# An adaLN block with attention and top-1 experts: GpSimd is drained between the two stages and behind the sends of the first five pairs

## The reference

```python
h = _layernorm(x, axis=-1) * (1 + ca) + sa
x = x + ga * _L0_attn_ref(h, w_qkv, w_swiglu, w_out)      # q, k, v, exp(k), cumsums, gated product
h = _layernorm(x, axis=-1) * (1 + cb) + sb
x = x + gb * _L0_ffn_ref(h, gate_w, w1, w2)

# _L0_ffn_ref, tokens of all batches, s = 4096, capacity = 320:
gate_logits = tokens.astype(jnp.float32) @ gate_w.T
combine_weights, sec_mask = _top1_router(gate_logits, capacity)
dispatch = jnp.einsum('sec,sd->ecd', sec_mask.astype(tokens.dtype), tokens)
h = jax.nn.gelu(jnp.einsum('ecd,edf->ecf', dispatch, w1))
expert_out = jnp.einsum('ecf,efd->ecd', h, w2)
out = jnp.einsum('sec,ecd->sd', combine_weights.astype(tokens.dtype), expert_out)
```

## Time and profile before

| | us |
|---|---|
| median of 3 runs | 220.8 (220.46 to 223.25) |
| profiled execution, its own time | 221.19 |
| profiled execution, span of the core | 219.4 |

### The profile page before, as it was taken

How to read it: one execution, slowest core, us unless ns; L and a number is a source line. 1 busy time by engine, 2 the same in 40 slices (tenths; PEclk the granted TensorE clock), 3 DMA queues, 4 the chain that set the end, 5 groups by cost and what they waited for, 6 DMA issues and landing times.

```text
span 219.4 us, 3971 instructions
## 1 busy us (share of the span) xinstructions
PE 189.2 (86%) x1155; PEld 153.1 (70%) x1155; DVE 152.5 (70%) x480; ACT 150.9 (69%) x438; POOL 101.8 (46%) x115
## 2 busy tenths in 40 slices
PE   7979989998998999698685688999999999999800
PEld 4858678687875888566474445887888988879700
DVE  3799799998999889999943407184766847576400
ACT  5398999999999999986535642585585864835000
POOL 6130132442046347556785550005575665767770
PEclk9999999999999999999975579999999999999975
DMA  4999999991104113412452217999969663310010
GB/s 137 307 343 358 359 344 321 341 276 56 51 0 142 57 48 114 150 72 76 172 179 94 78 39 192 363 356 357 335 207 348 213 186 101 137 37 28 24 37 0
DMA packets 37284, 38.60 MB, mean 176 GB/s; under 512 B 2591, under 2 KB 31334, under 8 KB 37264
## 3 DMA queue, kind: packets, MB, share of 16 engines
q1 hardware_dynamic: 33936, 31.29, 45.8%
q0 software_dynamic: 3328, 7.07, 9.0%
HBM read 19.19 MB, written 18.95 MB: 174 GB/s over the span
## 4 chain that ended last, share of the span: by engine, by line
PE 50%; DVE 15%; ACT 11%; issue 8%; POOL 6%; DMA 3%; SPq 1%; POOLq 1%; DVEq 0%; ACTq 0%
PE bank L1213 14%; PE bank L1199 11%; PE bank L981 5%; POOL out_dram L455 4%; ACT junk L491 3%; ACT ewkv L510 3%; PE bank L1033 2%; PE bank L1035 2%; DMA wmod<-in_L_wmod_dram 2%; POOL dispatched_rows L433 2%; DVE w1l L897 2%; PE bank L998 2%; PE bank L1170 2%; PE bank L1050 2%; PE bank L1019 2%
## 5 line engine op out<-in xcount | busy, mean ns | idle before, releaser
L455 POOL DMA_INDIRECT out_dram<-x_all,rest x40 | 42.5, 1062 | 40.7 <-DVE x_all L927 30.9
L433 POOL DMA_INDIRECT dispatched_rows<-rows,slot x32 | 31.5, 983 | 18.1 <-DVE slot L815 9.6
L652 ACT ACTIVATE HT<-bank 128x320 f32<-128x320 f32 x64 | 28.0, 438 | 10.2 <-PE bank L1199 9.8
L1213 PE MATMUL bank<-HT,w 128*128 128x320 f32 x112 | 32.4, 432 | 0.0
L1213 PEld LDWEIGHTS bank<-HT,w 128*128 128x128 f32 x112 | 20.6, 189 | 6.7
L1199 PE MATMUL bank<-xth,w1h 128*128 128x320 f32 x64 | 22.6, 354 | 0.2 <-DVE xtl L903 0.2
L897 DVE TENSOR_TENSOR w1l<-w,w1h 128x1024 fp32r<-128x1024 f32 x8 | 16.2, 2031 | 6.9 <-DMA dispatched_rows<-rows,slot 6.9
L946 DVE COPY OT<-bank 128x320 f32<-128x320 f32 x14 | 6.9, 492 | 18.5 <-PE bank L1213 18.5
L1199 PE MATMUL bank<-xth,w1l 128*128 128x320 f32 x64 | 19.8, 309 | 0.0
L1199 PE MATMUL bank<-xtl,w1h 128*128 128x320 f32 x64 | 19.8, 309 | 0.0
L491 ACT ACTIVATE junk<-bank 128x128 f32<-128x128 f32 x64 | 16.6, 290 | 2.6 <-PE bank L981 2.6
(11 more groups left out here) (163 smaller groups left out, 475.2 us busy)
## 6 DMA issues: line engine op xcount, KB each, us to landing
w<-in_L_ffn_w_dram SPq DMA_DIRECT2D x16, 512.0 KB, 8.1
dispatched_rows<-blank SPq DMA_DIRECT2D x8, 965.0 KB, 12.5
rest<-dispatched_rows SPq DMA_DIRECT2D x8, 645.0 KB, 6.0
hin<-dispatched_rows SPq DMA_DIRECT2D x7, 320.0 KB, 7.0
x_all<-in_L_attn_x_dram SPq DMA_DIRECT2D x8, 256.0 KB, 4.6
rows<-gb_row SPq DMA_DIRECT2D x8, 256.0 KB, 6.7
out_dram<-rows SPq DMA_DIRECT2D x8, 256.0 KB, 2.3
out_dram<-x_all,rest POOLq DMA_INDIRECT x40, 2.6
```

Source lines behind the costliest of these rows:

```text
L433: pool.indirect_dma_start(out=disp_d, out_offset=bass.IndirectOffsetOnAxis(ap=slot[:, b, j:j + 1], axis=0), in_=rows[:, b, j, :], in_offse ...
L455: pool.indirect_dma_start(out=out_d.rearrange("b t d -> (b t) d"), out_offset=bass.IndirectOffsetOnAxis(ap=rest[i % RING][:, n, C_TOK - D: ...
L652: act.activation(HT[e][:, f, :], ps_h[c % HB][:, 0:CAP], ACT.Gelu_apprx_tanh).then_inc(h_done, 1)
L1213: last = pe.matmul(ps_o[e], w2[i % RING][:, e, f, :], HT[e][:, f, :], start=(f == 0), stop=(f == NF - 1))
```

## The change

After the last scatter GpSimd now waits, besides the x1 rows, for the landing of all scatters, and then executes a drain. A further drain stands behind the five sends of each of the pairs 0 to 4 (i < SPLIT - 1 = 5). A drain holds GpSimd's program until it has finished; what stands behind it on the engine comes after. Pairs 5, 6 and 7 have none. Nothing else is changed: the instructions of all engines and their order stay the same.

```diff
             scatter(4); count_seen(5); scatter(5); count_seen(6); scatter(6); scatter(7)
 
             pool.wait_ge(x1_out, 16 * NB)
+            pool.wait_ge(scattered, 16 * NB * NJ)
+            pool.drain()
 
             last_token = pool.to_reg(NTOK - 1)
...
             for i in range(NPAIR):
                 for part, n0, n1 in parts(i):
                     send_tiles(part, i, n0, n1)
+                if i < SPLIT - 1:
+                    pool.drain()
```

## The result

The changed kernel takes 1.0084 times as long as the one before, with a 95% interval of 1.0047 to 1.0121: 0.8% slower, where I forecast 222.4 against 220.8 us, 0.7% slower. The medians of 20 runs each are 223.62 us with the change and 222.95 before; they hold disturbed executions too, which the ratio leaves out.

A forecast was written before the change was run, and what follows sets the result against it. GpSimd's sends from pair 5 and its last drain were taken to bound the end. Later sends +5.7 to +7.0 and the drain -4.6 made +1.65 us: 222.8 profiled, 222.4 forecast against 220.8, range 215.9 to 227.

The forecast's parts named there:

- What sets the end: End of the program: GpSimd's 10.04 us drain ends the time, and from pair 5 on GpSimd's sends bound it.
- The first drain: After the last scatter: 32 DMAs cost 2.6 us, all hidden in 19.7 us of GpSimd idle time.
- A portion for each DMA: In every GpSimd drain: work of 0.083 us (5.96/72) for each indirect DMA since the last drain.
- rival (b): Every drain: constant 4.83 us after landing, end some 27 us later, 248; chance 0.08, smaller constant above 2% 0.13.
- The wait for the landing: Drains behind pairs 0 to 4: each waits for the landing, then needs some 0.1 us; later sends +5.7 to +7.0.
- Rival (a): Drains behind pairs: portions for each DMA without waiting for landing; cost 0, gain 4.6 us, 216.2 us; chance 0.22.
- The places: First sends of pairs 1 to 5: delayed pair by pair, pair 5 at 200.05 to 201.3 instead of 193.39 us.
- The end: Last drain: ends 1.3 us after the last generation instead of 5.96, gain 4.6; later sends cost 5.7 to 7.0.
- A first loss of 3.1 us is never made good: Pairs 1 to 5: a pair takes about 9.7 us where TensorE allows 8.91, so the first delay stays.
- Rival (c): End of program: long end belongs to being the last drain, or drains are weightless; 221 to 222 us, chance 0.07.

The follow-up runs named there:

- the first four experiments: Four edits of the changed kernel: scatter drain only; landing waits without drains; extra drains after landings; drains behind scatters, pairs 3, 4. Kernel before: median 234.5 us.
- pairs 3 and 4: Changed kernel with only the drain after the scatters and those behind pairs 3 and 4; ratio 0.9886 (0.9741 to 1.0030) to the kernel before.
- drains with everything landed: Changed kernel, second drain after the scatters' drain; after the last pair a landing wait and drain replace the five; 0.083 us per send, 0.034 us empty drain.

## Why the prediction came out right, point by point

**What sets the end** was right: GpSimd's last drain, and from pair 5 on its sends. With the first drain alone the stretch from the first send to the end is 2.64 us shorter, and the last drain 2.63.

**The first drain**: 2.6 us forecast, hidden; 2.68 measured, hidden.

**A portion for each DMA**: right, and 0.083 us is what the direct measurement gives. It was a division of 5.96 by 72, and nothing in the trace of before had excluded rival (b), the constant; an empty drain of 34 ns does, and the 0.24 us behind a landing. That the division held was not known when it was made.

**The wait for the landing**: right. Rival (a), a drain that doesn't wait for it, would have had pair 1 in place; it starts 3.2 us late. The wait alone, with no drain, gives the same places within 0.25 us.

**The places**, behind pair 0: pair 1 at 11.96 forecast, 12.06 measured; pair 2 at 22.6, 21.98; pair 3 at 31.8 to 33.0, 31.82; pair 4 at 41.0 to 41.7, 40.88; pair 5 at 50.3 to 51.5, 50.40. From a landing to the next start I had 0.96 us (0.1 and 0.86), it was 1.07 (0.24 and 0.83). The landing of pair 1's last send was too slow in my sum (3.2 us, it was 2.5). The sends held up by VectorE came where I had them for pairs 1 and 2; in pairs 3 and 4 there were three (1.61, 1.45 and 1.58 us), where my sum names one. The one of 1.45 us started inside L931 (192.94 to 193.77), the other two inside L901. So the places come out near partly because these errors go opposite ways.

**The end**: the term that was mis-sized. I had the last drain end 1.3 us after the last generation, it was 1.79, since I took the portions to run beside the landing and half of them run behind it. The gain is 4.17 us and not 4.6. The last generation ends 5.80 us later behind pair 0 than before, at the lower end of the forecast's 5.7 to 7.0. The two make +1.63, where the forecast had +1.65: two errors of 0.4 to 0.5 us in opposite directions, so that the sum came out to some hundredths is luck.

**"A first loss of 3.1 us is never made good"** holds for the changed kernel, in which every pair waits for its landing; it is no property of the pipeline. With a drain behind pair 0 only, the loss was gone at pair 4. What costs in the change are the landings behind all five pairs in a row, which bring every pair above the 8.91 us that TensorE sets (12.07, 9.92, 9.84, 9.06 and 9.52 us from start to start).

**Rival (c)**, that the long end belongs to being the last drain, or that drains weigh nothing, is out. The constant 12 ns of the Trainium skill's page "VectorE: DVE Perf Modes", section "The DRAIN you can't avoid", is of the size of the 34 ns of an empty drain on GpSimd, and off by two orders behind 32 or more indirect DMAs. At the end of the program VectorE's 330 ns don't fit it either.

## What to carry to other kernels

When a kernel issues many indirect DMAs from GpSimd, look at the end of the profile: a drain may stand there that works off all of them, here 0.083 us each. A drain of one's own moves this work to where GpSimd idles, and is free where the idle time is longer than the landing of the last DMA, the portions and the restart of 0.83 us together. The gap between stages is such a place. The 2.2 us between two pairs is not: the gap came to 2.2 us at best, before pair 3, and to 5.4 where the last send took 5.9 us to land. One more drain just ahead of the part that GpSimd bounds gives more than five: the first drain with that of pair 4 takes the time to 0.982 to 0.986 of before, with all five it is 1.008. Over the first drain alone that one gives some 1.2 us by the profiles; the ratios don't resolve it.

## What the runs showed of the hardware that I had not expected

- A drain on GpSimd with 15 DMAs in front, the last of them unlanded, ends 0.65 us after that landing, with 37 it is 1.56, with 25 1.07, with 20 0.86 and with 5 0.24: about half of its work for each DMA lies behind the last landing. With all landed it is 0.083 us for each, whether rows of 386 or 128 elements were moved.
- A send that starts inside VectorE's two-input instruction on SBUF ends 0.8 us after that instruction, so it can take up to 2.7 us in place of 0.97; one that starts 0.04 us ahead of it takes its 0.97. What a shift of a pair costs hangs on this phase, up to 1.75 us for one send.
- When the first four experiments ran, the kernel before had a median near 234 us, later 221 to 223. In three of these four profiles (the first drain alone, pairs 3 and 4, drains with everything landed) ScalarE idled for 5.4, 7.2 and 7.5 us near the end, with nothing that the profile names to wait for, and the last rows came late. These runs don't settle the reason.
